# A graph network on one core: the split node's row read from PSUM, and three Newton steps in place of four

## The chip, the cores and the metric

One core of a Trainium2 chip. The metric is the device time of one execution in microseconds; before the change the median of three runs is 10569.1 us (10568.56 to 10575.79).

## What is computed

Four blocks over one graph: 6250 nodes with 64 features, 200000 edges sorted by destination node. Each block is followed by a residual and a layer norm. Cut to what matters here:

```python
x = _layernorm(x + _L0_gnn_ref(x, edge_attr_64, src, dst, W, b))         # per-channel softmax over a node's edges
x = _layernorm(x + _L1_gnn_ref(x, edge_index, W1, b1, W2, b2))           # two GCN layers, 1/sqrt(degree) scales
x = _layernorm(x + _L2_gnn_ref(x, edge_attr_128, fc_w, ..., src, dst))   # CGCNN: batch norms, sigmoid * softplus
x = _layernorm(x + _L3_gnn_ref(x, edge_index, edge_attr_16, ...))        # two PNA layers, each as follows

h    = concatenate([x[src], edge_attr @ We + be]) @ Wpre + bpre
mean = segment_sum(h, dst) / max(cnt, 1)
mn   = where(cnt == 0, 0, segment_min(h, dst))
mx   = where(cnt == 0, 0, segment_max(h, dst))
out  = concatenate([x, agg, agg * amp]) @ Wpost + bpost                  # agg = [mean, mn, mx]
out  = relu(batch_norm(out @ Wlin + blin))
```

`_layernorm` and the batch norms need reciprocal square roots of variances, the GCN layers those of the degrees: 21 calls of one helper in all.

## The kernel before

The edges are cut into two halves of 98 blocks of 512; the two halves lie on partitions 0 to 63 and 64 to 127. The program makes seven passes: SOFT, GCN1, GCN2, STAT, MSG, PNA1, PNA2. In the edge passes POOL gathers source rows by indirect DMA (L601, eight a block), TensorE turns them to one feature a partition, DVE scans along the edges with masks that restart at each new destination (sum, minimum and maximum: `scan`, L1435), and the running values go to DRAM, to `runs3_d` (three values) or `runs1_d` (one). The value at a node's last edge is that node's result.

Then comes the pass's node phase. Nodes lie 128 to a tile, 49 tiles (`NT`). POOL fetches the row of each node's last edge, one indirect DMA a tile: 49 gathers into `feat` (L693), after all of the pass's rows are in DRAM. DVE works on four groups of tiles (12, 12, 12 and 13 tiles), and starts a group when its gathers have landed (`ends`, L1677: semaphores `s_endg`). `pipeline` (L1670) sets the order: in step t group t goes through the first stage, and group t - 1 through the second, and so on. Nothing else sets an order: each engine's program is written out, and semaphores join them. `link` (L1347) makes each DVE instruction wait for the one before it.

One node's edges can be split between the two halves. Its row in the first half is fetched once, over all partitions, into `row0` (192 values in SBUF: L537 on SP), and added to the node for which `flag` is 1. In the last two passes (PNA1, PNA2) `first_half` (L2042) prepares this for all 49 tiles at once, while POOL gathers: row times flag into `tab`, `tmp` and `tmp2` (L2050: sum, minimum, maximum), and for minimum and maximum a third operand of plus or minus 3e38 where the flag is 0 (L2052, L2053). `tab` is a tensor of its own; `tmp` and `tmp2` lie in `arena`. All are in SBUF. The stage `pna_aggregates` (L2030) then merges each group with the gathered rows (L2036) and scales it (L2038), three tensor-tensors each. TensorE multiplies the group, and `pna_post` (L2055) adds up the products from PSUM (L2057, L2058) and a bias (L2062). After group 3 come the batch norm's mean and variance (`batch_scale`, L1633), then the last stage, in PNA2 with a layer norm (`layer_norm`, L1611).

PSUM: `pn` has five banks of 512 columns. Edge passes use it for the scans' columns, node phases for the products; between the two it is free.

The node phase after GCN2 has no gathers of end rows. There POOL scatters 49 tiles of a table to DRAM (L669), a group as soon as DVE has written it, and goes on with the gathers of STAT.

The helper `rsqrt` (L1602) is a bit trick followed by Newton steps of three chained instructions each (L1607 to L1609):

```python
                link(TS(v.bitcast(i32), v.bitcast(i32), -0.5, float(0x5F3759DF), ALU.mult, ALU.add))
                for _ in range(4):
                    link(TT(t, half, v, ALU.mult))
                    link(TT(t, t, v, ALU.mult))
                    link(STT(v, t, 1.5, v, ALU.add, ALU.mult))
```

Of the kernel before, what the change touches and what calls it, by code (L numbers as in the profile page):

```python
# [17 lines left out]
N, E, F = 6250, 200000, 64  # L18
P = 128
NT = -(-N // P)  # L20
# [11 lines left out]
BIG = 3e38  # L32
# [61 lines left out]
def gnn_kernel(nc, x, src, dst, ea128, ea16, ea64, W0, b0, W1, b1, W2, b2, fcw, fcb, bn1w, bn1b,  # L94
               bn2w, bn2b, We, be, Wpre, bpre, Wpost, bpost, Wlin, blin, gamma, beta, out):
    f32, bf16, i32, u16 = mybir.dt.float32, mybir.dt.bfloat16, mybir.dt.int32, mybir.dt.uint16
    ALU, ACT, AX = mybir.AluOpType, mybir.ActivationFunctionType, mybir.AxisListType
# [12 lines left out]
    with ctx:  # L110
# [81 lines left out]
        row0 = sb("row0", [P, 3 * F])  # L192
        cnt, pre, endf, flag, full, dinv, amp, mu, var = (
            sb(n, [P, NT]) for n in ("cnt", "pre", "endf", "flag", "full", "dinv", "amp", "mu", "var"))
# [29 lines left out]
        pn = pb("pn", [P, 5, BLK])  # L224
# [335 lines left out]
        def _(g):  # L560
# [85 lines left out]
            for p in range(7):  # L646
# [45 lines left out]
                for w in range(NT):  # L692
                    g.indirect_dma_start(out=feat[:, w, F:F + k * F], out_offset=None, in_=r,  # L693
                                         in_offset=bass.IndirectOffsetOnAxis(ap=endi[:, w:w + 1], axis=0))\
                     .then_inc(s_endg[sum(w >= z for _, z in SPAN)], 16)
# [3 lines left out]
        def _(pe):  # L699
# [141 lines left out]
            def node_matmuls(*calls, between=None):  # L841
# [14 lines left out]
                def product(n):  # L856
                    job, gr, c = STEPS[n]
                    _, width, chunks, weight, cols = CALLS[JOBS[job][0]]
                    G = fill[job, gr]
                    pe.wait_ge(s_tc, n + 1)  # L860
                    if c == 0 and G >= 5:
                        pe.wait_ge(s_po, G - 4)
                    a, z = GROUPS[gr]
                    for m, (w, v) in enumerate(units(JOBS[job][0], gr)):
                        by = weight[0:F * (v - w), 0:v - w, :].rearrange("p t c -> p (t c)") if width == F else weight(c)
                        last = mm(pn[:, G % 5, (w - a) * cols:(v - a) * cols], aT[0:width * (v - w), n % 2, m * P:(m + 1) * P],
                                  by, start=(c == 0 and w == a), stop=(c == chunks - 1), skip_group_check=True)
                    last.then_inc(s_mm, 1)
# [473 lines left out]
        def _(dve):  # L1342
            V = nc.vector
            TT, TS, STT, SCAN = V.tensor_tensor, V.tensor_scalar, V.scalar_tensor_tensor, V.tensor_tensor_scan
            chain = 0

            def link(ins):  # L1347

                nonlocal chain
                chain += 1  # L1350
                ins.then_inc(s_dve, 1)
                dve.wait_ge(s_dve, chain)
# [213 lines left out]
            def edge_pass(p):  # L1566
# [22 lines left out]
            over_f = lambda a: a.unsqueeze(2).broadcast_to([P, a.shape[1], F])  # L1589
# [2 lines left out]
            part = lambda k: feat[:, :, k * F:(k + 1) * F]  # L1592
            by_squares = lambda a: a.rearrange("p w (n c) -> p w n c", n=2)
            runs_part = lambda k, a, z: feat[:, a:z, F:4 * F].rearrange("p w (n k c) -> p w k n c", n=2, k=3)[:, :, k - 1, :, :]
            row_part = lambda k, n: row0[:, :].rearrange("p (n k c) -> p k n c", n=2, k=3)[:, k - 1, :, :]\
                .unsqueeze(1).broadcast_to([P, n, 2, SQ])
            over_squares = lambda a: a.unsqueeze(2).unsqueeze(3).broadcast_to([P, a.shape[1], 2, SQ])

# [3 lines left out]
            def rsqrt(v, half, t):  # L1602

                link(TS(half, v, -0.5, None, ALU.mult))
                link(TS(v.bitcast(i32), v.bitcast(i32), -0.5, float(0x5F3759DF), ALU.mult, ALU.add))
                for _ in range(4):
                    link(TT(t, half, v, ALU.mult))  # L1607
                    link(TT(t, t, v, ALU.mult))
                    link(STT(v, t, 1.5, v, ALU.add, ALU.mult))  # L1609
# [83 lines left out]
            def table_free(p):  # L1693
                if p in TABLE:
                    dve.wait_ge(s_td, TABLE[p])

            def counts():
# [27 lines left out]
                dve.sem_inc(s_end, 1)  # L1725
                link(TS(dinv[:, :], cnt[:, :], 1.0, None, ALU.add))
                rsqrt(dinv[:, :], mu[:, :], var[:, :])
                link(TS(mu[:, :], cnt[:, :], 1.0, 1.0, ALU.max, ALU.add))
                ask_scalar()
# [312 lines left out]
            def first_half(p):  # L2042

                dve.wait_ge(s_r0, 16 * (READS.index(p) + 1))
                table_free(p)
                link(TS(mu[:, :], cnt[:, :], 1.0, None, ALU.max))
                link(V.reciprocal(mu[:, :], mu[:, :]))
                link(TT(mu[:, :], mu[:, :], full[:, :], ALU.mult))
                for k, to, sign in ((1, tab, 0.0), (2, tmp, -1.0), (3, tmp2, 1.0)):
                    link(TT(by_squares(to[:, :, :]), row_part(k, NT), over_squares(flag[:, :]), ALU.mult))  # L2050
                    if sign:
                        link(TS(var[:, :], flag[:, :], 1.0, sign * BIG, ALU.subtract, ALU.mult))  # L2052
                        link(TT(to[:, :, :], to[:, :, :], over_f(var[:, :]), ALU.add))  # L2053

            def pna_post(k, v):  # L2055
                def post(a, z, o):
# [57 lines left out]
```

## Time and profile before

| | |
|---|---|
| median of 3 runs | 10569.1 us (10568.56 to 10575.79) |
| profiled execution | 10570.1 us, span of the core 10568.4 us |
| busy | POOL 67%, DVE 63%, PE 52%, PE weight loads 42%, ACT 21% |
| granted TensorE clock, mean | 0.706 |
| node phases of the last two passes | 8285 to 8422 us and 10400 us to the end |

The span is the time from the first to the last instruction of the core; 1.7 us lie around it. A busy share is an average over passes with different limits, so it does not tell what bounds one of them. The chain of waits does: it is followed back from the last instruction, at each step to what released it. The timeline lists the instructions of an engine in order of time, with the idle time before each and what ended it. In a DMA_INDIRECT row of POOL the length is the time that POOL spends on issuing the DMA; its data land later.

### The profile page before, as it was taken

Reading aid. Unit: us, or ns where it says so; the run is one execution under the profiler, and the core shown is the slowest. Engines: PE = TensorE matmul, PEld = TensorE weight load, DVE = VectorE, ACT = ScalarE, POOL = GpSimd, SP = SyncE. Lnnn points to the kernel's source line nnn. Section 1 sums busy time; section 2 is a strip of 40 time slices with the busy share of each in tenths; the row PEclk is TensorE's granted clock in tenths of the full one; section 3 lists DMA queues with packets and bytes.
Section 4 is the critical chain, followed back from the end, with each engine's and each line's share of the span. In section 5 each row is a group of like instructions: output and inputs, shape, how many; then the busy total and the mean of one; then the engine's idle time right before and its main releaser. Section 6 shows DMA issues by size and latency. Waiting matters only on the chain.

```text
span 10568.4 us, 124127 instructions
## 1 busy us (share of the span) xinstructions
PE 5527.7 (52%) x33901; PEld 4454.6 (42%) x33999; DVE 6613.1 (63%) x9196; ACT 2250.9 (21%) x3204; POOL 7100.7 (67%) x7048
## 2 busy tenths in 40 slices
PE   4666656459886666666644423333333434333333
PEld 3444444348885555445522213333333333333333
DVE  6777777789913555555578855555555555555555
ACT  1111111148700111111158821111111111111111
POOL 6777777626604777777755537777777577777774
PEclk8777787679997888888855555556556655556566
DMA  8777777524486777777756625555555355555552
GB/s 182 195 196 194 196 197 197 149 91 206 194 341 219 233 236 237 240 233 234 238 185 203 203 64 125 124 125 124 126 124 126 74 126 124 126 123 126 125 126 67
DMA packets 2347310, 1784.10 MB, mean 169 GB/s; under 512 B 1805829, under 2 KB 1977610, under 8 KB 2342282
## 3 DMA queue, kind: packets, MB, share of 16 engines
q1 hardware_dynamic: 774743, 879.12, 25.3%
q10 hardware_dynamic: 1356944, 617.91, 21.4%
q0 software_dynamic: 215456, 284.72, 11.7%
q8 instruction: 119, 1.95, 0.1%
q14 instruction: 48, 0.39, 0.0%
HBM read 921.34 MB, written 861.11 MB: 169 GB/s over the span
## 4 chain that ended last, share of the span: by engine, by line
POOL 53%; issue 22%; DVE 12%; PE 5%; ACT 4%; DMA 2%; ACTq 1%; SPq 1%; POOLq 0%; DVEq 0%
POOL arena L601 52%; DVE obuf L1894 3%; ACT arena L1116 2%; POOL feat L693 2%; PE ph L927 2%; PE pn L927 1%; DVE neg L1894 1%; DVE pos L1894 1%; ACT obuf L1086 1%; DMA arena<-in_x_dram,idx_src 1%; ACTq L1089 1%; ACT arena L1122 1%; DVE work L1437 0%; DVE arena L1476 0%; PE pn L763 0%
## 5 line engine op out<-in xcount | busy, mean ns | idle before, releaser
L601 POOL DMA_INDIRECT arena<-table_d,idx_src x3136 | 2959.0, 944 | 1123.4 <-issue 955.4
L765 PE MATMUL pn<-work,wblk 128*128 128x128 f32 x3136 | 1049.9, 438 | 2386.3 <-DMA arena<-table_d,idx_src 2386.3
L765 PEld LDWEIGHTS pn<-work,wblk 128*128 128x128 f32 x3136 | 838.0, 327 | 2525.6 <-issue 1844.9
L601 POOL DMA_INDIRECT arena<-in_x_dram,idx_src x1568 | 1495.7, 954 | 514.5 <-issue 469.4
L601 POOL DMA_INDIRECT arena<-tsrc_d,idx_src x1568 | 1479.5, 944 | 477.9 <-issue 477.9
L1378 DVE TENSOR_SCALAR idx_src<-src_all 128x8 int32 (+1 forms) x784 | 147.9, 190 | 2317.9 <-PE pn L766 1590.1
L766 PE MATMUL pn<-ident,arena 128*128 128x128 f32 x4704 | 1375.3, 392 | 0.0
L766 PEld LDWEIGHTS pn<-ident,arena 128*128 128x128 f32 x4704 | 1177.1, 306 | 0.0
L1476 DVE STREAM_TRANSPOSE arena<-work 128x512 f32<-128x512 f32 x1568 | 991.4, 680 | 98.2 <-DVE work L1437 98.2
L1437 DVE TENSOR_TENSOR_SCAN work<-keep,work,pn 128x512 f32<-128x512 bf16 x588 | 752.8, 1280 | 245.4 <-PE ph L778 200.9
L755 PE MATMUL pn<-work,weT 128*128 128x512 f32 x784 | 552.0, 794 | 663.3 <-DMA arena<-tsrc_d,idx_src 634.0
L763 PE MATMUL pn<-ident,attr 128*128 128x128 f32 x1568 | 417.8, 359 | 520.6 <-DMA arena<-in_x_dram,idx_src 510.0
L610 POOL TENSOR_SCALAR arena<-feat,bnsc,bnbi 128x512 f32<-128x512 f32 x392 | 422.5, 1089 | 366.7 <-DMA feat<-total_d 366.6
L757 PEld LDWEIGHTS pn<-ident,arena 128*128 128x128 f32 x3136 | 508.1, 230 | 265.0 <-issue 265.0
L763 PEld LDWEIGHTS pn<-ident,attr 128*128 128x128 f32 x1568 | 333.6, 260 | 647.4 <-issue 560.0
L1109 ACT ACTIVATE work<-pe_ 128x1024 f32<-128x1024 f32 x196 | 200.7, 1024 | 1782.8 <-PE pe_ L736 1782.8
L1201 ACT ACTIVATE feat<-pn 128x784 bf16<-128x784 f32 x592 | 487.7, 825 | 120.9 <-PE pn L907 112.4
L757 PE MATMUL pn<-ident,arena 128*128 128x128 f32 x3136 | 497.4, 311 | 0.0
L1437 DVE TENSOR_TENSOR_SCAN work<-pe_,work 128x512 f32<-128x512 f32 x392 | 496.2, 1266 | 0.0
L1437 DVE TENSOR_TENSOR_SCAN work<-pos,work,pn 128x512 f32<-128x512 bf16 x392 | 492.0, 1255 | 0.0
L1437 DVE TENSOR_TENSOR_SCAN work<-neg,work,pn 128x512 f32<-128x512 bf16 x392 | 491.7, 1254 | 0.0
L755 PEld LDWEIGHTS pn<-work,weT 128*128 128x128 f32 x784 | 155.4, 247 | 708.4 <-issue 347.2
(402 smaller groups left out, 11166.3 us busy)
## 6 DMA issues: line engine op xcount, KB each, us to landing
runs_d<-arena ACTq DMA_DIRECT2D x2352, 192.0 KB
adj_d<-feat SPq DMA_DIRECT2D x37, 3136.0 KB, 10.8
seed_d<-nothing SPq DMA_DIRECT2D x392, 256.0 KB
arena<-seed_d SPq DMA_DIRECT2D x392, 256.0 KB, 6.8
attr<-in_edge_attr_dram SPq DMA_DIRECT2D x392, 256.0 KB
feat<-total_d SPq DMA_DIRECT2D x196, 512.0 KB
keep<-keep_d SPq DMA_DIRECT2D x588, 128.0 KB
feat<-adj_d SPq DMA_DIRECT2D x37, 1600.0 KB, 9.0
```

The source lines that it names most:

```text
L601: g.indirect_dma_start(out=to, out_offset=None, in_=table, in_offset=bass.IndirectOffsetOnAxis(ap=idx, axis=0))\
L610: g.tensor_scalar(zbuf[:, u, part * BLK:(part + 1) * BLK], totals[:, u, part * BLK:(part + 1) * BLK], bnsc[:, part:part + 1], bnbi[:, part ...
L755: mm(to, weT[:, :], eT[:, s, h * BLK:(h + 1) * BLK], start=True, stop=False, skip_group_check=True)
L757: last = mm(to[:, j:BLK:J], gat[:, u, j, h, :], ident[:, :], start=False, stop=True, skip_group_check=True)
L763: mm(to, attr[:, u % 2, j * P:(j + 1) * P], ident[:, :], start=True, stop=False, skip_group_check=True)
L765: mm(to, wblk[:, PNA.index(p), j, :], feat_to[u], start=True, stop=False, skip_group_check=True)
L766: last = mm(to, gat1[:, u, j * P:(j + 1) * P], ident[:, :], start=(p in (GCN1, GCN2)), stop=True, skip_group_check=True)
L927: last = mm(to[:, j * 3 * F:(j + 1) * 3 * F], adj[:, m % 2, j * NT + w, :], tsp[:, w, :], start=(k == 0), stop=(w == NT - 1), skip_group_c ...
L1201: A(adj[:, m % 2, :, g * GROUP:(g + 1) * GROUP].rearrange("p k (b n) -> p k b n", b=2), pn[:, 2 * (k % 2):2 * (k % 2) + 2, 0:4 * KC].rearr ...
L1437: return SCAN(res[:, s, k, 1:BLK + 1], mask, data, res[:, 1 - s, k, BLK:BLK + 1], ALU.mult if mul else ALU.add, ALU.add if mul else ALU.mi ...
L1476: last = V.transpose(to[:, k, :, :], of.rearrange("p (m c) -> p m c", c=SQ))
L1894: last = TT(to.rearrange("p n (c d) -> p n c d", d=2), pairs[:, m % 2, k, n * HOT:(n + 1) * HOT, :].unsqueeze(2).broadcast_to([P, HOT, wid ...
```

## The change

Two edits in DVE's program. `rsqrt` runs its Newton loop three times instead of four, in all 21 calls. And `first_half` first copies `row0` into PSUM (192 columns of `pn`), multiplies by the flag from there, and writes the operand of plus or minus 3e38 to another 49 columns of the same bank instead of to `var` in SBUF. Each of the five large tensor-tensors then has one input in PSUM and one in SBUF; their outputs stay where they were.

```diff
-            row_part = lambda k, n: row0[:, :].rearrange("p (n k c) -> p k n c", n=2, k=3)[:, k - 1, :, :]\
+            row_part = lambda k, n, row=row0[:, :]: row.rearrange("p (n k c) -> p k n c", n=2, k=3)[:, k - 1, :, :]\
                 .unsqueeze(1).broadcast_to([P, n, 2, SQ])
...
-                for _ in range(4):
+                for _ in range(3):
                     link(TT(t, half, v, ALU.mult))
                     link(TT(t, t, v, ALU.mult))
                     link(STT(v, t, 1.5, v, ALU.add, ALU.mult))
...
                 link(TT(mu[:, :], mu[:, :], full[:, :], ALU.mult))
+                row_ps, away = pn[:, 0, 0:3 * F], pn[:, 0, 4 * F:4 * F + NT]
+                link(V.tensor_copy(row_ps, row0[:, :]))
                 for k, to, sign in ((1, tab, 0.0), (2, tmp, -1.0), (3, tmp2, 1.0)):
-                    link(TT(by_squares(to[:, :, :]), row_part(k, NT), over_squares(flag[:, :]), ALU.mult))
+                    link(TT(by_squares(to[:, :, :]), row_part(k, NT, row_ps), over_squares(flag[:, :]), ALU.mult))
                     if sign:
-                        link(TS(var[:, :], flag[:, :], 1.0, sign * BIG, ALU.subtract, ALU.mult))
-                        link(TT(to[:, :, :], to[:, :, :], over_f(var[:, :]), ALU.add))
+                        link(TS(away, flag[:, :], 1.0, sign * BIG, ALU.subtract, ALU.mult))
+                        link(TT(to[:, :, :], to[:, :, :], over_f(away), ALU.add))
```

The order of the instructions on the other engines is the same. On DVE the program has 2211 instructions where it had 2272 (loop bodies once): 63 of the Newton steps are gone, two copies are new. The place of the copy, in `first_half` of PNA1 and PNA2 (a plus marks what is new or changed; lines are those of the changed kernel, `pn` is PSUM, `row` is `row0`):

```order
+L2050 COPY pn<-row 128x192
+L2052 TENSOR_TENSOR tab<-pn,flag 128x3136
+L2052 TENSOR_TENSOR arena<-pn,flag 128x3136
+L2054 TENSOR_SCALAR pn<-flag 128x49
+L2055 TENSOR_TENSOR arena<-arena,pn 128x3136
+L2052 TENSOR_TENSOR arena<-pn,flag 128x3136
+L2054 TENSOR_SCALAR pn<-flag 128x49
+L2055 TENSOR_TENSOR arena<-arena,pn 128x3136
 L2036 TENSOR_TENSOR tab<-feat,tab 128x768
 L2036 TENSOR_TENSOR arena<-feat,arena 128x768 x2
```

The seven that stood here had the same shapes, with `row` and `var` in the place of `pn`. Nothing has moved past another instruction.

## Rows read from the trace of the kernel before

**Rows 1.** The page, part 4: the chain that ended last

```profile
POOL 53%; issue 22%; DVE 12%; PE 5%; ACT 4%; DMA 2%; ACTq 1%; SPq 1%; POOLq 0%; DVEq 0%
```

**Rows 2.** Timeline, POOL, last node phase (start, length, ..., [idle before])

```profile
10400.53 0.94 POOL L693 DMA_INDIRECT feat<-runs_d,endi  x1 [16.98 <-DMA runs_d<-arena]
...
10404.28 3.61 POOL L693 DMA_INDIRECT feat<-runs_d,endi  x1 [0.30 <-issue]
...
10428.73 0.95 POOL L693 DMA_INDIRECT feat<-runs_d,endi  x1 [0.30 <-issue]
10429.98 1.65 POOL L693 DMA_INDIRECT feat<-runs_d,endi  x1 [0.30 <-issue]
...
10479.03 0.95 POOL L693 DMA_INDIRECT feat<-runs_d,endi  x1 [0.30 <-issue]
```

**Rows 3.** Timeline, DVE, the same stretch

```profile
10403.65 3.42 DVE L2050 TENSOR_TENSOR tab<-row,flag 128x3136 f32<-128x3136 f32 x1
...
10417.93 3.43 DVE L2053 TENSOR_TENSOR arena<-arena,var 128x3136 f32<-128x3136 f32 x1
10428.86 0.96 DVE L2036 TENSOR_TENSOR tab<-feat,tab 128x768 f32<-128x768 f32 x1 [7.50 <-DMA feat<-runs_d,endi]
...
10481.75 1.02 DVE L2036 TENSOR_TENSOR tab<-feat,tab 128x832 f32<-128x832 f32 x1 [8.99 <-DMA feat<-runs_d,endi]
```

**Rows 4.** Groups, POOL, 10404-10422, 8289-8307, 10430-10436, 8316-8319 (busy us, mean ns)

```profile
L693 POOL DMA_INDIRECT feat<-runs_d,endi x5 | 16.7, 3335 | 1.5 <-issue 1.5
...
L693 POOL DMA_INDIRECT feat<-runs_d,endi x5 | 16.7, 3332 | 1.5 <-issue 1.5
...
L693 POOL DMA_INDIRECT feat<-runs_d,endi x3 | 5.0, 1671 | 0.9 <-issue 0.9
...
L693 POOL DMA_INDIRECT feat<-runs_d,endi x2 | 3.2, 1616 | 0.6 <-issue 0.6
```

**Rows 5.** Groups by form, DVE; last row from the page

```profile
L2057 DVE TENSOR_TENSOR arena<-pn,amp 128x64 f32<-128x64 f32 x2 | 0.5, 226 | 0.2
...
L1646 DVE TENSOR_TENSOR nrow<-nrow,Bgamma 128x64 f32<-128x64 f32 x2 | 0.5, 225 | 0.1
...
L1437 DVE TENSOR_TENSOR_SCAN work<-keep,work,pn 128x512 f32<-128x512 bf16 x588 | 752.8, 1280 | 245.4 <-PE ph L778 200.9
```

**Rows 6.** Timeline, statistics pass: POOL, then DVE

```profile
4021.74 0.94 POOL L601 DMA_INDIRECT arena<-tsrc_d,idx_src  x1 [0.30 <-issue]
...
4021.51 1.29 DVE L1548 TENSOR_TENSOR obuf<-pn,work 128x512 f32<-128x512 f32 x2
```

**Rows 7.** Timeline, DVE, one Newton step in a layer norm

```profile
10525.87 0.17 DVE L1607 TENSOR_TENSOR pre<-mu,var 128x12 f32<-128x12 f32 x1
...
10526.49 0.17 DVE L1607 TENSOR_TENSOR pre<-mu,var 128x12 f32<-128x12 f32 x1
```

**Rows 8.** Source line L1607 (ns min/median/max, first and last start)

```profile
L1607 DVE TENSOR_TENSOR pre<-mu,var x64: 170/171/176, 2121.0 to 10562.2; 128x12 f32<-128x12 f32 x48, 128x13 f32<-128x13 f32 x16
L1607 DVE TENSOR_TENSOR nrow<-nrow x12: 224/226/226, 6227.3 to 10517.1; 128x64 f32<-128x64 f32 x12
L1607 DVE TENSOR_TENSOR var<-mu,dinv x4: 211/212/258, 2041.0 to 2043.3; 128x49 f32<-128x49 f32 x4
L1607 DVE TENSOR_TENSOR nrow<-col x4: 160/161/163, 5365.1 to 5366.9; 128x2 f32<-128x2 f32 x4
```

**Rows 9.** Chain of waits in two node phases (start, length)

```profile
2203.25 1.04 DVE xres L1621
...
6299.32 1.03 DVE xres L1621
```

**Rows 10.** Timeline, second neighbour-sum node phase: POOL, DVE

```profile
3310.39 1.05 POOL L669 DMA_INDIRECT seed_d<-feat,starti  x1 [35.42 <-DVEq L1668]
...
3359.59 0.98 POOL L669 DMA_INDIRECT seed_d<-feat,starti  x1 [0.30 <-issue]
...
3353.30 0.06 DVE L1567 MEMSET work<- 128x3 f32 x1 [0.28 <-DVE feat L1834]
```

## Prediction

> **What bounds the kernel now.** The page's chain of waits comes first [rows 1]: POOL carries 53% of it, DVE 12%, and 22% is issue time, most of it the 0.30 us between one indirect DMA of POOL and the next. So a microsecond of DVE counts only in two cases: where DVE itself is the chain, and where DVE makes POOL's indirect DMAs longer. The change touches DVE code of both kinds. I therefore read two timelines side by side in the node phase of the last pass, POOL's [rows 2] and DVE's [rows 3].
>
> POOL starts 49 gathers of end rows at 10400.53, each about 0.95 us with 0.30 us between them, a pitch of 1.249 us. The first one after 10404 takes 3.61 us. In that stretch DVE runs the five tensor-tensors of `first_half`, 3.42 us each, whose two inputs both lie in SBUF. Five gathers in a row are held: 16.68 us in all in the last pass and 16.66 us in the pass before [rows 4], where five free ones take 4.73 us. Each of the two passes loses 11.95 and 11.93 us to this. The two timelines also give the pattern. The gather of 10404.28 ends at 10407.89, 0.82 us after the tensor-tensor that ran when it started (10403.65 + 3.42). The gather of 10428.73 is not held (0.95 us) though a tensor-tensor starts 0.13 us after it; the next, started at 10429.98 inside a tensor-tensor, takes 1.65 us. So what decides is whether such an instruction is running within the first 0.13 us or so of the gather; if one is, the gather ends 0.82 us after it.
>
> These gathers are the chain. The last one starts at 10479.03, its row lands 2.72 us later, and DVE, idle since its third group, starts group 3 only then, at 10481.75 [rows 2, 3]. DVE had finished `first_half` at 10421.36, and even group 0 waited until 10428.86.
>
> **Part 1, the row in PSUM.** Two tensor-scalars of 128x49 now write to PSUM instead of SBUF, which I price at nothing (the copy's bounds cover them); added is one copy of 128x192. From 64 to 3136 elements a tensor-tensor grows by 1.041 ns an element (225 ns [rows 5], 3425 ns [rows 3]), so the copy is 0.225 + 128 x 0.00104 = 0.36 us, some 0.4 us with the gap. All of it is on DVE, under POOL's gathers: `first_half` now ends near 10421.8, when the 12 gathers of group 0, which would be in by 10400.53 + 11 x 1.249 + 2.72 = 10417.0, are there. So for group 0 DVE is late instead of POOL, for the others POOL stays late. If that cover were gone, the copy would cost 0.4 us a pass.
>
> Does a tensor-tensor take longer with one input in PSUM? Equal shapes say no: 226 ns with PSUM, 225 ns without, at 128x64 [rows 5]. The far bound is the scan, with mask in SBUF and data in PSUM, 1280 ns for 512 columns, 2.5 ns an element. That would make each of the five 7.84 us. I take no change.
>
> Does it still hold the gathers? In the statistics pass two tensor-tensors of the same kind, one input in PSUM and one in SBUF, run from 4021.51 to 4022.80; the gather started inside them, at 4021.74, takes 0.94 us [rows 6]. So the five should hold nothing, and 11.95 and 11.93 us come back. The bound below is no gain at all. The Trainium skill, SBUF — State Buffer, "Who interferes with whom", says that a DVE instruction with at most one SBUF input, outside the two-port modes, does not contend with GpSimd; by that rule the sum is the same.
>
> What is late next is group 0's own work. Its six tensor-tensors (two SBUF inputs, 0.96 us each and about 0.035 us apart) now start at about 10421.8 and no longer on a landing. Going through the pattern above with gathers every 1.249 us from 10400.53, the gather of 10421.76 ends at 10423.6, the next at 10425.6, the third at 10427.5: three held, 2.30 us lost. Before, group 0 held three for 3 x (1.671 - 0.945) = 2.18 us in the last pass, but only two for 2 x (1.616 - 0.945) = 1.34 us in the pass before [rows 4], where the same arithmetic gives 2.30 as well. So the net is 11.95 + 2.18 - 2.30 = 11.8 us in the last pass, and 11.93 + 1.34 - 2.30 = 11.0 us before it. Groups 1 and 2 start on landings, so that their holds move along with POOL unchanged. Sum of part 1: **22.8 us**. If group 0 held between one and four gathers (0.8 us each), it would be 20.4 to 26.
>
> **Part 2, one Newton step less.** A step is three chained instructions. At 128x12 they follow each other every 0.21 us, 0.62 us a step [rows 7]. The other shapes have 225 ns at 128x64, about 0.215 at 128x49 and 0.161 at 128x2 [rows 8]; with 0.035 us between them that is 0.78, 0.75 and 0.59 us a step. There are 21 roots: 16 in the layer norms (12 of 128x12, 4 of 128x13), 3 of 128x64 in the batch scales, one of 128x49, one of 128x2. Where are they the chain?
> - Node phase after the first pass: the chain of waits runs through DVE up to 2203.25 [rows 9]. One 128x49, three and one layer norms: 0.75 + 3 x 0.62 + 0.63 = 3.2 us.
> - After the second neighbour-sum pass: POOL starts its 49 scatters at 3310.39, when the tables of group 0 stand, and never waits again: it starts group 3 at 3359.59, 6 us after DVE is done with the phase at 3353.30 [rows 10]. Only the layer norms ahead of POOL's start count, groups 0 and 1: 1.24 us. The other two shift DVE's two-input instructions against the scatters; through the same pattern (with 0.98 us a scatter) I find 0.6 us more hold. I take 0.6 us, between 0 and 1.3.
> - Batch scale of the edge statistics: 0.59 us, with every engine waiting for it.
> - Message pass: the chain is DVE to 6299.32 [rows 9]: 0.78 + 1.86 + 0.63 = 3.3 us.
> - First of the last two passes: 0.78 us, its batch scale. Last pass: 0.78 + 1.86 + 0.63 = 3.3 us, at the very end with nothing beside it.
>
> Sum of part 2: 3.2 + 0.6 + 0.6 + 3.3 + 0.8 + 3.3 = **11.8 us**, between 11 and 12.5.
>
> **Sum.** 22.8 + 11.8 = 34.6 us. The profiled execution took 10570.1 us, 1.0 above the median shown, so 10535.5 us on its own time and 10534.5 on the median. I say 10535 us, 0.33% less. A measurement of this kernel tells about 0.2% from no change, 21 us.
>
> **Rivals.**
> - *The gathers stay held.* What holds them might not be the second SBUF input but something that both forms share, such as the large SBUF output or the zero-stride reads over 3136 elements. The statistics pass speaks against it: its tensor-tensors write SBUF too. For it speaks only that no row has this long broadcast form with a PSUM input. Then part 1 gives nothing and part 2 stays: 10569.1 - 11.8 = 10557 us. The same page of the Trainium skill says of `tensor_tensor` that it takes only the read interface of the shared pair while descriptor generation needs the write interface (it calls this inferred), so that such an instruction would not stall DMAs; by that, part 1 has nothing to win. The trace disagrees with it: 3.61 us against 0.95 us. Chance 0.07.
> - *A part is held.* The small instructions around or a longer hold behind group 0 leave half of part 1: 10569.1 - 11.4 - 11.8 = 10546 us. Chance 0.03.
> - *DVE becomes the bound, and it gets slower.* If PSUM makes the five instructions much longer, `first_half` ends late, and groups 0 to 2 (six tensor-tensors each, 5.97 us, and for two groups 3.5 us of products behind them) reach group 3's landing at 10469.9. DVE would be free at 10421.8 + 3 x 5.97 + 2 x 3.5 = 10446.7, so 23 us are hidden: 4.6 us more on each of the five. The scan's rate would add 4.4 us, still hidden. Above 7 us more (three times as long) the pass gets longer than before, and at 13.7 us each (four times) both passes lose 16.4 us, which outweighs part 2 by 21: 10590 us. Rows 5 speak against it. Chance 0.02.
>
> **How the numbers follow.** The forecast has 0.88. Its own bounds are 31.4 us (20.4 + 11.0) and 38.5 us (26 + 12.5), 10531 to 10538; the three executions shown spread over 7 us, with one that much above the others, so I reach to 10528 and 10545. The rivals hold 0.12 and stay outside but for a part of the second. Faster by over 0.2% means below 10548: the forecast and most of the second rival, 0.90. Within 0.2%: the first rival and the rest, 0.08. Slower: 0.02.
>
> **What would show it.** In the two last node phases every gather that starts during `first_half` takes 0.95 us, the five tensor-tensors stay at 3.42 us, group 0 starts right behind them with three gathers held, and group 3 starts 11 to 12 us earlier after the phase's first gather. The tail from the last batch scale is 3.3 us shorter, with 48 instead of 64 of each Newton instruction in the layer norms. Wrong would be: gathers of over 3 us under a tensor-tensor with a PSUM input, tensor-tensors above 4 us, or a wait of DVE or POOL in these phases that takes the place of the saved time.

## The result and the profile after

The changed kernel took 10539.3 us, median of 7 runs (10532.11 to 10541.54), beside 10569.1 us for the kernel before (7 runs, 10566.9 to 10577.38): a ratio of 0.9969, with a 95% interval of 0.9957 to 0.9981. That is 29.8 us less, by the interval 20 to 45 us, and faster by more than the 0.2% that a measurement can tell. The forecast of 10535 us was off by 4.3 us and its range of 10528 to 10545 held the time.

The profiled execution of the changed kernel took 10537.6 us (span 10535.9, granted clock 0.707 as before), 32.5 us less than the profiled execution of before. The page's part 4, the chain that ended last, hardly moved against [rows 1]; 0.3 per cent can't show in rounded shares:

```profile
POOL 54%; issue 22%; DVE 11%; PE 5%; ACT 4%; DMA 2%; ACTq 1%; SPq 1%; POOLq 0%; DVEq 0%
```

The node phase of the last pass shows the change. Here is DVE's timeline of the changed kernel there, the answer to [rows 3] (start, length, line, names, shapes, [idle before]):

```profile
10386.82 0.36 DVE L2050 COPY pn<-row 128x192 f32<-128x192 f32 x1
10387.22 3.42 DVE L2052 TENSOR_TENSOR tab<-pn,flag 128x3136 f32<-128x3136 f32 x1
...
10401.53 3.42 DVE L2055 TENSOR_TENSOR arena<-arena,pn 128x3136 f32<-128x3136 f32 x1
10404.99 0.96 DVE L2036 TENSOR_TENSOR tab<-feat,tab 128x768 f32<-128x768 f32 x1
...
10452.78 1.02 DVE L2036 TENSOR_TENSOR tab<-feat,tab 128x832 f32<-128x832 f32 x1 [9.00 <-DMA feat<-runs_d,endi]
```

And POOL's timeline of the same stretch, the answer to [rows 2]:

```profile
10383.69 0.94 POOL L693 DMA_INDIRECT feat<-runs_d,endi  x1 [16.74 <-DMA runs_d<-arena]
...
10387.44 0.95 POOL L693 DMA_INDIRECT feat<-runs_d,endi  x1 [0.30 <-issue]
...
10404.94 0.94 POOL L693 DMA_INDIRECT feat<-runs_d,endi  x1 [0.30 <-issue]
10406.18 1.57 POOL L693 DMA_INDIRECT feat<-runs_d,endi  x1 [0.30 <-issue]
10408.06 1.69 POOL L693 DMA_INDIRECT feat<-runs_d,endi  x1 [0.30 <-issue]
10410.05 1.68 POOL L693 DMA_INDIRECT feat<-runs_d,endi  x1 [0.30 <-issue]
...
10450.06 0.95 POOL L693 DMA_INDIRECT feat<-runs_d,endi  x1 [0.30 <-issue]
```

The gather of 10387.44 starts 0.22 us into the first long tensor-tensor and takes 0.95 us; before, the one in that place took 3.61 us. All gathers up to the one of 10404.94 are free (0.94 to 0.95 us). DVE goes from `first_half` straight into group 0 (no idle time at 10404.99), and then three gathers are held. Group 3 starts 69.09 us after the phase's first gather (10452.78 - 10383.69), and started 81.22 us after it before (10481.75 - 10400.53): 12.13 us less in this pass. In the pass before it, it is 69.18 against 80.15 us: 10.97 us less. DVE still waits 9.00 us for the landing of group 3, as before (8.99 us).

The durations are as expected. Source lines L693, L2052, L2055 and L2050 of the changed kernel (ns min/median/max, first and last start):

```profile
L693 POOL DMA_INDIRECT feat<-runs_d,endi x196: 940/946/1712, 2040.6 to 10450.1; - x196
L2052 DVE TENSOR_TENSOR arena<-pn,flag x4: 3424/3424/3424, 8288.1 to 10397.8; 128x3136 f32<-128x3136 f32 x4
L2055 DVE TENSOR_TENSOR arena<-arena,pn x4: 3420/3420/3420, 8291.8 to 10401.5; 128x3136 f32<-128x3136 f32 x4
L2050 DVE COPY pn<-row x2: 362/362/363, 8284.2 to 10386.8; 128x192 f32<-128x192 f32 x2
```

The longest of the 196 gathers took 1712 ns; in the kernel before it was 3613 ns. With an input in PSUM the five tensor-tensors keep their 3.42 us, and the copy takes the 0.36 us worked out for it.

To see where the time went, I cut both traces (and all later ones) at the same instructions. In us:

| stretch | before | after | difference | forecast |
|---|---|---|---|---|
| first pass: first gather of end rows to last layer norm | 162.75 | 159.28 | -3.47 | -3.2 |
| GCN1 pass | 682.96 | 683.75 | +0.79 | 0 |
| GCN2 node phase: first L1819 to first scatter | 29.59 | 28.37 | -1.22 | -1.24 |
| first scatter to first gather of STAT | 67.14 | 68.24 | +1.10 | +0.6 |
| STAT pass, to the statistics | 1975.27 | 1979.93 | +4.66 | 0 |
| edge statistics' batch scale | 15.45 | 14.86 | -0.59 | -0.6 |
| message pass: first gather of end rows to L1643 | 85.81 | 83.93 | -1.88 | 0 |
| L1643 to the first gather of PNA1 | 84.87 | 82.15 | -2.72 | -3.3 |
| PNA1: first gather of end rows to L1643 | 112.11 | 100.67 | -11.44 | -11.0 |
| its L1643 to the first gather of PNA2 | 29.11 | 28.03 | -1.08 | -0.8 |
| PNA2: first gather of end rows to L1643 | 113.05 | 100.64 | -12.41 | -11.8 |
| L1643 to the last layer norm | 49.28 | 46.03 | -3.25 | -3.3 |

GCN1, STAT and the message pass up to L1643 hold nothing that the change touches; the nine other rows, which it sets, sum to -35.1 us. STAT takes 4.66 us longer in this execution of the changed kernel. The experiments tell whether the change did that.

### The profile page after: what moved, and what is told of

Same layout as the page of the kernel before. It is cut to its first block, busy times and chain, and to the rows that moved or that the text cites. A ratio compares the mean times of both kernels' runs of the same rounds, so it can differ in the third digit from the quotient of the medians.

```text
span 10535.9 us, 124164 instructions
## 1 busy us (share of the span) xinstructions
PE 5539.9 (53%) x33999; PEld 4445.4 (42%) x33999; DVE 6599.3 (63%) x9135; ACT 2249.6 (21%) x3204; POOL 7064.1 (67%) x7048
## 4 chain that ended last, share of the span: by engine, by line
POOL 54%; issue 22%; DVE 11%; PE 5%; ACT 4%; DMA 2%; ACTq 1%; SPq 1%; POOLq 0%; DVEq 0%
POOL arena L601 52%; DVE obuf L1894 3%; ACT arena L1116 2%; PE ph L927 2%; POOL feat L693 1%; PE pn L927 1%; DVE neg L1894 1%; DVE pos L1894 1%; ACT obuf L1086 1%; ACTq L1089 1%; DMA arena<-in_x_dram,idx_src 1%; ACT arena L1122 1%; DVE work L1437 0%; PE pn L866 0%; DVE arena L1476 0%
```

## The experiments

My theory is the prediction's: five gathers in each of the last two passes lose their hold because no running instruction of DVE has two SBUF inputs any more, and every Newton step on the chain gives its own length. Its rivals are that the reduced Newton steps bring most of it, that only part of the PSUM operands matter, and that something other than the hold sets the phases. The kernels below ran on two chips, the first four on one and the others on the other. There the kernel before takes 10610.27 us (22 runs), and 10614.33 and 10614.26 us (18 and 9 runs), 41 to 45 us more than beside the result, so each is held against the runs of before beside it, and against the times of the stretches.

### One part at a time

The first kernel has only the Newton steps, with the row in SBUF:

```
-                row_ps, away = pn[:, 0, 0:3 * F], pn[:, 0, 4 * F:4 * F + NT]
-                link(V.tensor_copy(row_ps, row0[:, :]))
-                    link(TT(by_squares(to[:, :, :]), row_part(k, NT, row_ps), over_squares(flag[:, :]), ALU.mult))
+                    link(TT(by_squares(to[:, :, :]), row_part(k, NT), over_squares(flag[:, :]), ALU.mult))
```

(and `var` in place of `away`).

> Three Newton steps, the row still read from SBUF. If the two parts are independent and the roots count only where DVE is the chain: 11.8 us less than the kernel before (11 to 12.5), the five gathers during first_half still held (16.7 us for five), the tail from the last batch scale's second mean to the last layer norm 46.0 us against 49.3. If the statistics pass (1975.3 us from its first gather to bn_aggr in the trace before, 1979.9 in the trace after) is lengthened by the change itself, by the earlier start that the shorter roots give it, it shows about 1980 us here too; if its length differs from execution to execution, it can be anything between 1975 and 1980, in this and in every other run.

Measured: 10597.64 us against 10610.27, ratio 0.9989 (0.998 to 0.9998), 12.6 us less. The second kernel has only the PSUM operands, with four steps:

```
-                for _ in range(3):
+                for _ in range(4):
```

> Row and third operand in PSUM, four Newton steps. Second-input theory: no gather is held during first_half, first gather to group 3 takes 70.2 us in the first and 69.1 us in the second of the last two node phases (81.2 before), 22.8 us less than the kernel before in all (20.4 to 26). If instead the large SBUF outputs or the broadcast reads hold the gathers, nothing is gained. The statistics pass starts at the same time as in the kernel before, so if the shift of its start lengthens it, it is back at 1975 us here.

Measured: 10586.15 us, ratio 0.9977 (0.9968 to 0.9986), 24.1 us less. The third is the change itself, unaltered, to have it on the same chip.

> The changed kernel once more, for its time beside the two parts on one chip and for a second trace. Between 30 and 35 us less than the kernel before. If the lost 4.7 us of the statistics pass are the change's own, this trace shows about 1980 us from the first gather of that pass to bn_aggr again; if they are chance, another number.

Measured: 10575.38 us, ratio 0.9969 (0.9957 to 0.9981), 34.9 us less. The expectations were 11.8, 22.8, and 30 to 35 us. The totals alone can't confirm tenths (their intervals are 19 to 25 us wide); the traces can. The gathers of the PNA1 node phase, grouped on POOL while `first_half` runs (line, names, count | busy us, mean ns | idle), the first kernel:

```profile
L693 POOL DMA_INDIRECT feat<-runs_d,endi x5 | 16.7, 3334 | 1.5 <-issue 1.5
```

and the second kernel, from the phase's first gather on:

```profile
L693 POOL DMA_INDIRECT feat<-runs_d,endi x17 | 16.1, 946 | 21.7 <-DMA runs_d<-arena 16.8 <-issue 4.9
```

With three Newton steps and the row in SBUF the five gathers are held exactly as in [rows 4]. With four steps and the row in PSUM seventeen in a row are free. Group 3 starts 68.5 and 69.0 us after the phase's first gather in this kernel; the expectation's 70.2 us for the first of the two had been read at that group's second merge. The stretches divide the same way: from the first gather of end rows to L1643, PNA1 and PNA2 take 111.45 and 112.56 us in the first kernel (before: 112.11 and 113.05), 100.28 and 100.73 us in the second. From L1643 to the last layer norm it is 46.00 us in the first and 49.26 us in the second. So the two parts are independent, each of the size of its term.

### Which of the operands holds

The next kernel keeps the row in PSUM, but leaves the third operand of the two additions in SBUF:

```
-                        link(TS(away, flag[:, :], 1.0, sign * BIG, ALU.subtract, ALU.mult))
-                        link(TT(to[:, :, :], to[:, :, :], over_f(away), ALU.add))
+                        link(TS(var[:, :], flag[:, :], 1.0, sign * BIG, ALU.subtract, ALU.mult))
+                        link(TT(to[:, :, :], to[:, :, :], over_f(var[:, :]), ALU.add))
```

> The changed kernel, but the operand of plus or minus 3e38 stays in SBUF: of the five long tensor-tensors three (times flag) have one SBUF input, two (the additions) have two. Second-input theory: exactly the gathers that start during an addition are held, one or two for each, each ending 0.82 us after it; the gathers under the three multiplications take 0.95 us. With a gather every 1.25 us each addition of 3.42 us costs 2.2 to 3.2 us, so 5 to 6 us per node phase against the change, 10 to 12 us in all. If output or broadcast were what holds them, all five or none would hold.

Measured: one run, 10583.75 us, 26.5 us less than before, so 8.4 us behind the change. DVE's timeline in its PNA1 node phase, products and additions in turn:

```profile
8325.35 3.42 DVE L2052 TENSOR_TENSOR arena<-pn,flag 128x3136 f32<-128x3136 f32 x1
8328.81 0.19 DVE L2054 TENSOR_SCALAR var<-flag 128x49 f32<-128x49 f32 x1
8329.03 3.43 DVE L2055 TENSOR_TENSOR arena<-arena,var 128x3136 f32<-128x3136 f32 x1
8332.49 3.42 DVE L2052 TENSOR_TENSOR arena<-pn,flag 128x3136 f32<-128x3136 f32 x1
8335.95 0.19 DVE L2054 TENSOR_SCALAR var<-flag 128x49 f32<-128x49 f32 x1
8336.17 3.43 DVE L2055 TENSOR_TENSOR arena<-arena,var 128x3136 f32<-128x3136 f32 x1
```

and POOL's timeline beside it:

```profile
8328.38 0.95 POOL L693 DMA_INDIRECT feat<-runs_d,endi  x1 [0.30 <-issue]
8329.63 3.65 POOL L693 DMA_INDIRECT feat<-runs_d,endi  x1 [0.30 <-issue]
8333.58 0.94 POOL L693 DMA_INDIRECT feat<-runs_d,endi  x1 [0.30 <-issue]
8334.83 0.95 POOL L693 DMA_INDIRECT feat<-runs_d,endi  x1 [0.30 <-issue]
8336.08 0.95 POOL L693 DMA_INDIRECT feat<-runs_d,endi  x1 [0.30 <-issue]
8337.33 3.09 POOL L693 DMA_INDIRECT feat<-runs_d,endi  x1 [0.30 <-issue]
```

This is the cleanest view of the hold, since both forms alternate: both write 3136 elements to SBUF, take 3.42 to 3.43 us and read an operand over zero strides. The gather of 8333.58 starts inside a product with the row in PSUM and is free. The gathers of 8329.63 and 8337.33 start inside additions of two SBUF inputs, and end at 8333.28 and 8340.42, 0.82 us behind the end of their addition (8329.03 + 3.43 = 8332.46, 8336.17 + 3.43 = 8339.60). The gather of 8336.08 is free although an addition starts 0.09 us after it. That rejects the rival by which the large output or the zero-stride form held the gathers. An addition holds exactly one gather, which costs (3.65 - 0.95) + (3.09 - 0.95) = 4.8 us in this phase. The phase to L1643 took 105.28 us, 4.7 us more than in the change on the same chip (100.58); in PNA2 it was 105.49 against 101.10, 4.4 us more. Together that is 9.1 us, a little under the 10 to 12 expected, because each addition holds one gather and not sometimes two.

### How much work the landings hide

By the prediction's account `first_half` now costs nothing as long as group 3 still waits for its landing. The next two kernels run its five tensor-tensors twice and three times, to the same values:

```
-                for k, to, sign in ((1, tab, 0.0), (2, tmp, -1.0), (3, tmp2, 1.0)):
+                for k, to, sign in ((1, tab, 0.0), (2, tmp, -1.0), (3, tmp2, 1.0)) * 2:
```

> The changed kernel with the five PSUM tensor-tensors of first_half done twice (same result): 17.8 us more of DVE work in each of the last two node phases. Cover theory: group 3 of the gathers lands 69 to 70 us after the first gather, and DVE needs 21.3 + 17.8 + 3 x 6 + 2 x 3.5 = 64 us up to there, so all of it stays hidden: within 2 us of the change in all. If DVE were the bound already, it would cost up to 36 us.

> The same done three times: 35.6 us more of DVE work in each of the two phases, which is more than the cover. Cover theory: DVE comes free for group 3 only 21.3 + 35.6 + 25 = 82 us after the first gather, against a landing at 69 to 70: 12 to 13 us more a phase, 24 to 26 us more than the change in all, about the time of a kernel with three Newton steps and the row in SBUF. If the cover were larger than I think, less; if smaller, the run that does it twice shows it.

Measured: twice 10580.03 us against 10614.33, ratio 0.9965 (0.9952 to 0.9978), 34.3 us less, that is, 35.6 us of added work on DVE (17.8 us a pass) at no cost that the totals show. Three times: 10610.92 us, ratio 0.9997 (0.9988 to 1.0006), 3.4 us less, so the next 35.6 us cost 31 by the medians. Group 3's first instruction in PNA1 and then in PNA2, DVE's timeline of the kernel with two:

```profile
8398.40 1.03 DVE L2036 TENSOR_TENSOR tab<-feat,tab 128x832 f32<-128x832 f32 x1 [0.53 <-DMA feat<-runs_d,endi]
...
10499.59 1.02 DVE L2036 TENSOR_TENSOR tab<-feat,tab 128x832 f32<-128x832 f32 x1 [1.71 <-DMA feat<-runs_d,endi]
```

and with three, the node phase of PNA2 from the end of `first_half`:

```profile
10488.55 3.42 DVE L2055 TENSOR_TENSOR arena<-arena,pn 128x3136 f32<-128x3136 f32 x1
10492.01 0.96 DVE L2036 TENSOR_TENSOR tab<-feat,tab 128x768 f32<-128x768 f32 x1
...
10498.08 0.96 DVE L2036 TENSOR_TENSOR tab<-feat,tab 128x768 f32<-128x768 f32 x1 [0.15 <-DVE feat L2038]
...
10505.80 0.42 DVE L2059 TENSOR_TENSOR arena<-pn,amp 128x256 f32<-128x256 f32 x1 [0.76 <-PE pn L866]
...
10508.08 0.42 DVE L2059 TENSOR_TENSOR arena<-pn,amp 128x256 f32<-128x256 f32 x1 [1.40 <-PE pn L866]
...
10519.77 1.03 DVE L2036 TENSOR_TENSOR tab<-feat,tab 128x832 f32<-128x832 f32 x1
```

With two, group 3 still starts on a landing, after idle times of only 0.53 and 1.71 us. With three there is no idle time: DVE sets the phase, which is the state of the rival "DVE becomes the bound". The cover can now be read off. Groups 0 to 2 take 27.8 us of DVE (10519.77 - 10492.01), not the 25 us that the prediction added up, mostly since DVE waits for TensorE's products of group 0 behind the merge of group 1 (0.76 and 1.40 us above). In the change `first_half` ends at 10404.99 and group 3 lands at 10452.78, so 47.8 - 27.8 = 20.0 us are hidden. Two repetitions add 35.6 us on DVE; 35.6 - 20.0 = 15.6 us, and group 3 starts 85.0 us after the phase's first gather instead of 69.1, 15.9 us later.

With two repetitions the stretches show more than that the added work costs nothing. To L1643 the two phases take 98.09 and 96.22 us, against 100.58 and 101.10 us in the repeated change and 100.67 and 100.64 us in the first. One reason is in the same theory: the later merges meet the gathers otherwise, eight gathers are held instead of nine, and group 3 starts 67.7 and 68.2 us after the first gather. The rest comes behind group 3. In the last pass, over the 10.3 us before L1643, the change has a granted clock of 0.83 and waits 4.65 us for TensorE at L1643; with two repetitions it is 1.00 over 8.6 us and 2.97 us. No run tests this second part. The total doesn't show the gain: in the profiled execution the first edge pass alone took 13.1 us longer than in the change (2053.7 us up to its first gather of end rows, against 2040.6). So the later work of DVE is not neutral, and a total within 2 us of the change, as expected, doesn't prove that nothing moved. With three repetitions the phases take 113.99 and 114.34 us, 13 to 14 us more than the change, as expected.

### What the bank costs, and can more operands move

The row needs bank 0 of `pn`, into which TensorE also writes products of every fifth group. The next kernel leaves bank 0 to the row for good, and gives the products the other four, a possible price of any layout that keeps operands in PSUM:

```
-                    if c == 0 and G >= 5:
-                        pe.wait_ge(s_po, G - 4)
+                    if c == 0 and G >= 4:
+                        pe.wait_ge(s_po, G - 3)
-                        last = mm(pn[:, G % 5, (w - a) * cols:(v - a) * cols], ...
+                        last = mm(pn[:, 1 + G % 4, (w - a) * cols:(v - a) * cols], ...
```

> The changed kernel with the products of the node phases in four PSUM banks instead of five (bank 0 left free). Prices the bank that the next kernel needs. Three tiles' worth of products have one bank each, three banks a group; with four, TensorE runs one product ahead less. Expected 0 to 3 us more, in the phases that are DVE's (after the first pass and the message pass).

Measured: 10583.45 us, ratio 0.997 (0.9958 to 0.9982), 30.9 us less than before, so 4.0 us worse than the change's 34.9 by medians on two chips, where 0 to 3 us were expected. The intervals are wider than that difference. The traces place 2.4 us of it: the first pass's node phase takes 160.34 us (159.27 in the change), the table phase of GCN2 29.70 us (28.36).

With a bank free, the scales that the merge and the message phase read can lie in PSUM too, so that fewer instructions have two SBUF inputs:

```
+            mu_ps, full_ps, flag_ps = (pn[:, 0, 5 * F + n * NT:5 * F + (n + 1) * NT] for n in range(3))
...
-                link(TT(t, over_w(row0[:, 0:F], z - a), over_f(flag[:, a:z]), ALU.mult))
+                link(TT(t, over_w(row0[:, 0:F], z - a), over_f(flag_ps[:, a:z]), ALU.mult))
-                link(TT(o, o, over_f(full[:, a:z]), ALU.mult))
+                link(TT(o, o, over_f(full_ps[:, a:z]), ALU.mult))
...
-                    merged = ((1, tab, ALU.add, mu), (2, tmp, ALU.min, full), (3, tmp2, ALU.max, full))
+                    merged = ((1, tab, ALU.add, mu_ps), (2, tmp, ALU.min, full_ps), (3, tmp2, ALU.max, full_ps))
```

> The changed kernel with the per-node scales, too, in PSUM (bank 0, products in the other four): full and mu in the last two aggregations, flag and full after the message pass. Of the six tensor-tensors of a group three keep two SBUF inputs; after the message pass one of three. Second-input theory with the 0.82 us rule: two gathers held a group instead of three in the last two phases (0.75 us less for each of three groups, 4.5 us in both), and one shorter hold instead of two after the message pass (about 1 us for each of three groups, 3 us). Together 7 us less than the change, minus what the run with four banks costs.

Measured: 10573.14 us, ratio 0.9961 (0.9948 to 0.9975), 41.2 us less than before. Both node phases are 4 to 5 us shorter than the change's (96.10 and 96.71 us to L1643, against 100.58 and 101.10); mostly one gather of a group is held for long instead of three. That is 8.9 us in both where 4.5 were expected, since the expectation let two be held. In the message phase more was held than I had thought: it takes 82.71 us to L1643, 1.2 to 3.1 us less than the change, where 3 were expected. DVE's timeline there:

```profile
6208.09 0.95 DVE L1690 TENSOR_TENSOR arena<-row,pn 128x768 f32<-128x768 f32 x1 [21.12 <-DMA feat<-runs_d,endi]
6209.08 0.96 DVE L1691 TENSOR_TENSOR feat<-feat,arena 128x768 f32<-128x768 f32 x1
6210.07 0.95 DVE L1692 TENSOR_TENSOR feat<-feat,pn 128x768 f32<-128x768 f32 x1
6211.06 0.56 DVE L2007 COPY arena<-feat 128x768 f32<-128x768 f32 x1
```

and POOL's:

```profile
6208.05 0.94 POOL L693 DMA_INDIRECT feat<-runs_d,endi  x1 [0.30 <-issue]
6209.30 1.55 POOL L693 DMA_INDIRECT feat<-runs_d,endi  x1 [0.30 <-issue]
6211.16 1.27 POOL L693 DMA_INDIRECT feat<-runs_d,endi  x1 [0.30 <-issue]
6212.73 0.94 POOL L693 DMA_INDIRECT feat<-runs_d,endi  x1 [0.30 <-issue]
```

L1691 has two SBUF inputs, and the gather of 6209.30 ends at 6210.85, 0.81 us behind its end (6209.08 + 0.96). Then the gather of 6211.16, inside a plain copy with a single SBUF input, ends at 6212.43, again 0.81 us behind the copy's end. So such a copy from SBUF to SBUF holds too. It runs at 0.56 us for 768 columns, faster than the 0.95 us of the tensor-tensors of the same size.

The last version takes both lessons. The bank is chosen by the group's call, so that only the calls from the message pass on do with four banks, and in the message phase the last product is written to its destination directly, without the copy:

```
+        BANK = [G % 5 if JOBS[job][0] < 5 else 1 + G % 4 for G, (job, _) in enumerate(FILLS)]
+        FREED = [max((n for n in range(G) if BANK[n] == BANK[G]), default=-1) + 1 for G in range(len(FILLS))]
...
-                link(TT(o, o, over_f(full_ps[:, a:z]), ALU.mult))
+                link(TT(t, o, over_f(full_ps[:, a:z]), ALU.mult))
...
-            link(V.tensor_copy(tmp[:, a:z, :], part(1)[:, a:z, :]))
```

> The kernel with the scales in PSUM, but with five banks again for the products of the first five multiplications (first node phase and second neighbour-sum phase) and four only where bank 0 holds the scales; and after the message pass the last product is written to its place at once instead of being copied there (the SBUF-to-SBUF copy of 0.56 us held a gather in the run with the scales). Against that run: 1.1 and 1.3 us back for the banks, one hold less in each of three groups (0.33 us each, 1.0 us) and the copy of the last group (1.05 us), so 4.5 us less; 10 to 11 us less than the change, 45 us less than the kernel before.

Measured: 10570.36 us against 10614.26, ratio 0.9959 (0.9946 to 0.9973), 43.9 us less than before and by medians 9 us less than the change, where 45 and 10 to 11 were expected; against the version before it the medians give 2.7 us for the 4.5 expected. The intervals overlap, so all of this rests on the stretches. Those are: first pass 159.28 us and GCN2 28.37 us, both back at the change's values; the message phase to L1643 81.62 us, where the change has 83.93 and 85.82; the last two 95.94 and 96.59 us. POOL's timeline in its message phase has one held gather at the start of a group, three in all where the version before had six:

```profile
6196.92 1.49 POOL L695 DMA_INDIRECT feat<-runs_d,endi  x1 [0.31 <-issue]
6198.71 0.95 POOL L695 DMA_INDIRECT feat<-runs_d,endi  x1 [0.30 <-issue]
...
6212.44 1.40 POOL L695 DMA_INDIRECT feat<-runs_d,endi  x1 [0.30 <-issue]
```

### What differs by itself

Beside the last version the kernel before was profiled once more, to see how far a stretch moves that nothing touches.

> The kernel before once more, for a second trace. If the differences that the change does not explain are chance (statistics pass of 1975 us in the trace before, 1979.9 and 1983.0 us in two of the change; from the message pass's first end-row gather to its second mean 85.8 us against 83.9 and 85.8), they can fall either way here; the stretches that the change sets stay: 162.8 us for the first node phase, 112.1 and 113.1 us from the first gather to the second mean in the last two node phases, 49.3 us at the end.

Measured: 10617.49 us. Its STAT pass takes 1979.25 us, where the first trace of before has 1975.27. None of the other kernels edits that pass, and four of them have 1975.4 to 1975.6 us, one 1978.06, three 1980.99 to 1982.88; the changed kernel has 1979.93 in one trace and 1982.96 in the other. So the 4.66 us that STAT took longer in the compared pair lie inside what the same code does from one execution to the next, and don't belong to the change.

## Why the prediction held, point by point

**Five gathers free in each pass: right.** They came back with 11.95 and 11.93 us, as the longest gather of 1712 ns and the pitch up to 10404.94 show. Reading one pair of rows side by side [rows 2, 3], then checking the form with PSUM in another pass [rows 6], was enough. The Trainium skill, SBUF — State Buffer, "Who interferes with whom", says that a DVE instruction with two SBUF inputs contends with a GpSimd instruction that reads SBUF. In a parenthesis, called inferred, it also says that `tensor_tensor` takes only the read interface while descriptor generation needs the write interface, so that it would not stall such DMAs. By that, part 1 would have given nothing; the runs disagree, with 3.65 against 0.94 us in one timeline. The Trainium skill, SBUF — State Buffer, "A bandwidth-pool intuition that's wrong (but worth ruling out)", says that such a DMA is blocked until about 115 ns behind DVE's end. The wait for DVE's end agrees; the delay behind it is 0.81 to 0.83 us here.

**No slower with PSUM, copy 0.36 us: right.** 3424 and 3420 ns, and 362 ns.

**Group 0 holds three gathers: right, with its cost a little high.** The prediction went through the pattern and took 2.30 us. In PNA2 it is (1.57 + 1.69 + 1.68) - 3 x 0.945 = 2.1 us. The step that was off is the pattern's front edge: the prediction let a tensor-tensor hold a gather if it ran within the gather's first 0.13 us or so, and so counted the gather just ahead of group 0 as the first held. That one (10404.94) takes 0.94 us, though group 0's first merge starts 0.05 us behind it (10404.99). The three after it are held. Group 3 starts 12.13 and 10.97 us earlier, against 11.8 and 11.0 forecast. By the stretches to L1643 the pair gives 12.41 and 11.44 us.

**Newton steps where they are the chain: right.** First pass 3.47 us (3.2), edge statistics 0.59 us (0.6), end 3.25 us (3.3), PNA1's batch scale 1.08 us (0.8), message pass 2.72 us (3.3). The stretch of the message term takes 81.52 to 82.28 us in the traces with three steps and 84.75 to 84.98 us in those with four, so the term is 2.5 to 3.5 us.

**The layer norms ahead of the scatters: right in kind, mis-sized.** The term was 0.6 us, as 1.24 us won before POOL's start less 0.6 us of more hold. Won were 1.22 us; lost were 1.10 us, in longer scatters. The group of all 49 scatters, before and then after:

```profile
L669 POOL DMA_INDIRECT seed_d<-feat,starti x49 | 51.0, 1041 | 50.0 <-DVEq L1668 35.7 <-issue 14.3
```

```profile
L669 POOL DMA_INDIRECT seed_d<-feat,starti x49 | 52.1, 1064 | 48.8 <-DVEq L1668 34.5 <-issue 14.3
```

POOL's wait ahead of them fell by 1.2 us, and its own busy time rose by 1.1 us. It isn't chance. Every trace with three steps has 68.2 to 68.5 us for that stretch, and every one with four has 67.1 or 67.2, the PSUM-only kernel among them. So the net was 0.1 us, inside the 0 to 1.3 that the prediction allowed. The step that was mis-sized is the 0.6 us of more hold, which measured 1.1 us. The prediction got it from the pattern with the wrong front edge; how much of the 0.5 us that explains was not worked out.

**DVE as the bound: rejected at this size, with its price corrected.** The condition was right (three repetitions bring it about), but the cover from the end of `first_half` is 20.0 us and not 23, mostly because groups 0 to 2 need 27.8 us and not 24.9. At the rival's four times the length, DVE would have been some 3 us later in each pass than it said (an estimate from these sums).

**The total.** 34.6 us forecast, 29.8 us on the result's chip, 34.9 us where the change was repeated. The nine stretches that the change sets gave 35.1 us in the trace pair. The 4.8 us between forecast and result are not a missing term that any trace shows: a stretch that the change doesn't touch (STAT) moves by up to 7.6 us between executions, and the result's own interval of 20 to 45 us holds both. What they are in the medians stays open. That the total came within 4.3 us of the forecast is in part luck; the stretches, with 35.1 us for 34.6, are what bears the sum out.

## What to carry to other kernels

Where GpSimd issues indirect DMAs on the critical path, look for those longer than the free ones and lay DVE's timeline beside them. In every trace here, a long tensor-tensor with both inputs in SBUF held a gather that started inside it until its own end. A small broadcast operand copied once to PSUM (0.36 us) removed that and left the tensor-tensors at 3.42 us. The bank that it takes should be one that TensorE doesn't need: four banks instead of five cost 2.4 us in two stretches. Work added under a landing cost nothing here while it stayed under the 20 us that the landings hid, which repeating the work measures directly; but it shifts what comes after it, and the stretches have to be looked at, not the total alone.

## What the runs showed of the hardware that was not expected

- A held gather ends 0.81 to 0.83 us behind the end of the DVE instruction that holds it, whatever it had waited, and a free one takes 0.94 to 0.95 us. In the twelve traces 462 gathers of end rows take over 1.0 us, and 461 of them end so, each begun while such an instruction ran.
- What decides is which of the two started first. In 42 cases a tensor-tensor with two SBUF inputs started within 0.13 us behind a gather, and none of these gathers took over 0.95 us. In 12 cases it had started up to 0.04 us ahead, and the gather was free as well; the latest start that held one was 0.053 us ahead. In those 12 the tensor-tensor itself was longer, 0.99 to 1.03 us instead of 0.96 for 768 elements. So the 0.13 us between 0.95 and 0.82 are not a time in which DVE can still get ahead of the gather, as the prediction had it. What happens inside a gather no run shows.
- A float32 copy of 128x768 from SBUF to SBUF holds a gather as well (1.27 to 1.29 us instead of 0.94, in 13 cases), though it has one input. It runs at 0.56 us. A tensor-scalar of that shape from SBUF to SBUF (L1792 of the changed kernel, 0.56 us too) does the same in the first pass, to all 24 gathers that began inside one.
- A tensor-tensor over 3136 elements is as long with one input in PSUM (3424 and 3420 ns) as with two in SBUF (3.42 to 3.43 us).
- The same code differs from one place to another. The GCN1 pass takes 683 us in the two traces taken beside the result and 718 to 731 us in all ten others, from two chips. That is of the size of the whole difference of 41 to 45 us. Of the other stretches that the experiments leave alone, the first edge pass is the widest: 2039 to 2042 us up to the first gather of end rows in ten traces, 2048.1 in the PSUM-only kernel's and 2053.7 in the one with two repetitions. STAT lies within 8 us. In the chain of waits between 2400 and 3000 us GCN1 runs mostly through DVE beside the result, and through POOL and issue time in the later trace; in these two lines (shares by line, cut off by the view; the kernel before each time) the same kernel has another bound:

```profile
by line: DVE obuf L1894 43.6%; DVE neg L1894 17.0%; DVE pos L1894 13.7%; PE ph L927 5.8%; issue 3.7%; PE pn L927 3.5%; DVE work L1905 1.0%; DVE work L1908 1.0%; DVE arena L1940 1.0%; DVE arena L1886 0.9%; DMA sum_d<-arena,dlo 0.9%; DVE aren
```

```profile
by line: issue 38.9%; POOL sum_d L634 24.1%; POOL arena L625 10.6%; DMA arena<-near_d,dlo 5.8%; DVE obuf L1894 5.2%; PE ph L927 2.7%; DVE neg L1894 1.9%; DVE pos L1894 1.7%; DMA sum_d<-arena,dlo 0.9%; PE pn L866 0.8%; DVE work L1878 0.6%; D
```

Why is open; nothing was tried on it, and that the chip makes the difference is likely but not shown. It is a reason to compare a kernel only with runs of before taken beside it.
